# Inverse norms per sequence in ten GpSimd operations, and new instruction lists for a two-layer transformer kernel

## The reference

```
ada = silu(cond) @ Wada.T + bada          # gamma1, gamma2, scale1, scale2, shift1, shift2
qn = q / max(norm(q), 1e-12) * exp(min(scale_mul_log, log(100)))   # one factor per head
kn = k / max(norm(k), 1e-12)
o  = softmax(qn @ kn.T + attn_bias) @ v
x  = x + (o @ Wproj.T + bproj) * gamma1
x  = x + (gelu(ln(x)*(scale2+1)+shift2 @ Wfc1.T + bfc1) @ Wfc2.T + bfc2) * gamma2
```

## Time and profile before

| | before |
|---|---|
| median of 3 runs | 340.05 us |
| the 3 runs | 339.28, 340.05, 344.35 us |
| profiled execution, own time | 337.69 us |
| profiled execution, span from first to last instruction | 335.9 us |
| mean granted TensorE clock | 0.98 |
| busy PE, DVE, ACT, POOL | 301.0, 221.2, 207.0, 149.7 us |

### The profile page before, as it was taken

How to read it: one execution, slowest core, us unless ns; L and a number is a source line. 1 busy time by engine, 2 the same in 40 slices (tenths; PEclk the granted TensorE clock), 3 DMA queues, 4 the chain that set the end, 5 groups by cost and what they waited for, 6 DMA issues and landing times.

```text
span 335.9 us, 7317 instructions
## 1 busy us (share of the span) xinstructions
PE 301.0 (90%) x2516; PEld 251.2 (75%) x2516; DVE 221.2 (66%) x535; ACT 207.0 (62%) x698; POOL 149.7 (45%) x264
## 2 busy tenths in 40 slices
PE   7797766799987989986999999999979999999986
PEld 7396555576866866765797878889768898988985
DVE  3854788688777889858868688664453883543441
ACT  3454639989992899887699576836571433632110
POOL 3446959764475453688325138522214512202000
PEclk9599999999997999999999999999979999999999
DMA  6998223000000020000001000000000000000000
GB/s 200 283 338 283 83 92 126 1 2 3 1 2 2 0 65 0 3 1 3 0 2 64 0 2 2 2 0 18 8 12 0 2 0 18 17 2 19 16 0 33
DMA packets 14037, 14.30 MB, mean 43 GB/s; under 512 B 1569, under 2 KB 12961, under 8 KB 14001
## 3 DMA queue, kind: packets, MB, share of 16 engines
q1 hardware_dynamic: 14000, 13.83, 13.1%
HBM read 12.76 MB, written 1.06 MB: 41 GB/s over the span
## 4 chain that ended last, share of the span: by engine, by line
PE 54%; DVE 16%; POOL 9%; issue 8%; ACT 8%; DMA 3%; SPq 1%; DVEq 0%; POOLq 0%; ACTq 0%
PE ps_linear L1562 15%; PE ps_hidden L1366 6%; PE ps_hidden L1368 5%; PE ps_hidden L1367 5%; PE ps_linear L1532 3%; PE ps_probs L1497 3%; ACT z L980 3%; DMA stage<-in_Wqkv 3%; DVE z L1254 2%; PE ps_scores L1486 2%; PE ps_turn L1402 2%; DVE neg_max L1265 2%; PE ps_output L1513 2%; PE ps_turn L1396 1%; PE ps_scores L1481 1%
## 5 line engine op out<-in xcount | busy, mean ns | idle before, releaser
L980 ACT ACTIVATE z<-z,neg_max 128x128 f32<-128x128 f32 x128 | 49.6, 391 | 13.1 <-DVE neg_max L1265 12.9
L822 POOL TENSOR_TENSOR h_lo<-xn,h_hi 128x256 fp32r<-128x256 f32 x32 | 24.1, 756 | 40.9 <-ACT h_hi L944 40.8
L1000 ACT ACTIVATE probsT<-ps_probs 128x512 f32<-128x512 f32 x48 | 28.4, 591 | 11.3 <-PE ps_probs L1497 11.2
L1497 PE MATMUL ps_probs<-ident,z 128*128 128x128 f32 x192 | 29.9, 278 | 3.7 <-ACT probsT L1000 2.6
L1562 PE MATMUL ps_linear<-WdT,g_h 128*128 128x256 f32 x128 | 29.5, 383 | 1.4 <-DVE g_h L1337 1.3
L1036 ACT ACTIVATE g_a<-ps_hidden 128x256 f32<-128x256 f32 x32 | 12.4, 387 | 29.0 <-PE ps_hidden L1368 28.6
L874 POOL TENSOR_TENSOR z<-z,row_inv 128x512 f32<-128x512 f32 x16 | 17.0, 1062 | 28.1 <-DVE row_inv L1279 28.1
L1562 PE MATMUL ps_linear<-Wfc2T,g_h 128*128 128x256 f32 x128 | 29.4, 382 | 0.0
L1497 PEld LDWEIGHTS ps_probs<-ident,z 128*128 128x128 f32 x192 | 21.7, 141 | 7.7 <-ACT probsT L1000 3.7
L1562 PEld LDWEIGHTS ps_linear<-WdT,g_h 128*128 128x128 f32 x128 | 23.7, 190 | 5.0 <-issue 1.4
L984 ACT ACTIVATE z<-ps_scores,neg_max 128x128 f32<-128x128 f32 x64 | 22.6, 368 | 7.8 <-DVE neg_max L1271 7.8
(11 more groups left out here) (166 smaller groups left out, 897.5 us busy)
## 6 DMA issues: line engine op xcount, KB each, us to landing
gamma<-gamma_scratch SPq DMA_DIRECT2D x8, 256.0 KB, 3.8
stage<-in_Wada SPq DMA_DIRECT2D x6, 256.0 KB, 4.0
stage<-in_Wqkv SPq DMA_DIRECT2D x4, 256.0 KB, 4.9
X<-in_x SPq DMA_DIRECT2D x4, 256.0 KB, 5.3
stage<-in_Wfc SPq DMA_DIRECT2D x4, 256.0 KB, 5.8
Wfc2T<-in_Wfc SPq DMA_DIRECT2D x1, 1024.0 KB, 7.5
WdT<-in_Wd SPq DMA_DIRECT2D x1, 1024.0 KB, 8.5
stage<-in_Wg SPq DMA_DIRECT2D x4, 256.0 KB, 2.7
```

The source lines that it names most:

```text
L822: pool.tensor_tensor(h_lo[:, m, :, j * P:(j + 1) * P], h_full[:, m, j, :, :], h_hi[:, m, :, j * P:(j + 1) * P].bitcast(F32), ALU.subtract) ...
L980: ins = act.activation(z[:, d, u, :], z[:, d, u, :], ACT.Exp, bias=neg_max[:, d, u:u + 1], accum_out=head_sum[:, n % 2, t, u, b:b + 1])
L1000: act.activation(probsT[:, G % 2, :, :], bank_of(key)[:, :].rearrange("p (u q) -> p u q", u=4), ACT.Copy).then_inc(is_freed(key)[0], 1)
L1497: ins = pe.transpose(bank[:, u * P:(u + 1) * P], z[:, G % DEEP, u, :], ident[:, :])
```

## The change

First, `qk_root_` works on one sequence (32 columns) and takes ten operations: one of third order (six operations) and one Newton round (four). Second, the head scale moves into its input: `head_scale` now holds exp(-2 log scale) for q and 1 for k, and the floor operation on DVE multiplies by it, so that the inverse root comes out with the scale inside. The first `qk_sum` on DVE therefore waits for `head_exp` on ACT, which POOL waited for before. A sequence's inverse norms are no longer bound to those of its partner.

Third, the play's numbers change: a load 0.95 for 0.75, the DMA latency 3.0 for 2.2, other durations of a few steps, and all due times. Fourth, some steps are held back in the play until what reads them can follow: a QK product until its buffer is free, a V product until the last values that read its buffer, a transpose until the last scores of its kind, a projection until its gamma has come; and steps of one name keep their order.

```diff
+MIN_LOG_SCALE = -20.0
...
-NEWTON = 3
...
-GROUP_US = [-39.5, -38.5]
...
+GROUP_US = [-6.5, -554.0]
+ATT_BASE = [-3890.5, -875.0, -147.0, -2073.0, 1326.5, -859.0, 551.0, 1266.0]
+MLP_BASE = [374.5, 2507.0, -998.5, -79.5, -1090.5, -2655.5, 3581.0, -1914.5]
...
-LATENCY = 2.2
+LATENCY = 3.0
...
-    add(("sines",), "ACT", 4.0, [("angles", 2)], at=2)
-    add(("load_small",), "SP", 4.0, at=-3.3)
+        add(("angles", i), "DVE", (1.4, 1.25, 0.7)[i], [("cond_silu",)] + ([("angles", i - 1)] if i else []), at=2)
+    add(("sines",), "ACT", 2.0, [("angles", 2)], at=2)
+    add(("load_small",), "SP", 4.5, at=-3.3)
     add(("head_clip",), "DVE", 0.2, [("load_small",)], at=1)
-    add(("head_exp",), "ACT", 0.25, [("head_clip",), ("cond_tanh",)], at=1)
...
-        add(("load", c), "SP", 0.75, [user] if c >= STAGE else [], at=due)
+        add(("load", c), "SP", 0.95, [user] if c >= STAGE else [], at=due)
...
-                add(("qk_product", n), "PE", 1.55, [("norm_low", "a", n), w_ready], "linear", at=a)
+                add(("qk_product", n), "PE", 1.55, [("norm_low", "a", n), w_ready, last_j.get(("qk", j))], "linear", at=a)
...
-                add(("v_product", n), "PE", 0.8, [("norm_low", "a", n), ("qk_product", n), ("weight_low", LAST_CHUNK["Wqkv"])], "linear", at=a + 0.1)
+                add(("v_product", n), "PE", 0.8, [("norm_low", "a", n), ("qk_product", n), ("weight_low", LAST_CHUNK["Wqkv"]), last_values], "linear", at=a + 0.1)
...
-                add(("qk_sum", n), "DVE", 1.25, [("qk_square", n), last_j.get(("qk", j))], at=a)
+                add(("qk_sum", n), "DVE", 1.3, [("qk_square", n), ("head_exp",), last_j.get(("qk", j))], at=a)
+                add(("qk_root", n), "Pool", 3.5, [("qk_sum", n)], at=a)
+                add(("qk_scale", n), "DVE", 1.0, [("qk_root", n)], at=a)
...
-                    add(("qk_root", r), "Pool", 5.0, [("qk_sum", m) for m in ns] + [("head_exp",)], at=a)
...
-            add(("project", n), "PE", 0.95, [("attn_copy", n), ("load_whole", "Wproj" if layer == 0 else "Wo"), prev(("project",), n)], "linear", at=g)
+            add(("project", n), "PE", 0.95, [("attn_copy", n), ("load_whole", "Wproj" if layer == 0 else "Wo"), prev(("project",), n)]
+                + ([("gamma_load", pair)] if layer == 0 else []), "linear", at=g)
             add(("residual", "a", n), "DVE", 0.335, [("project", n), prev(("residual", "a"), n)]
...
+    last = {}
+    for key, step in steps.items():
+        name = key[:2] if len(key) > 2 and isinstance(key[1], str) else key[0]
+        if name not in ("load", "load_x", "load_whole", "gamma_load", "modulate", "modulated", "store"):
+            if name in last and last[name] not in step[2]:
+                step[2].append(last[name])
+            last[name] = key
...
+            pool.memset(head_scale[:, H0:2 * H0], 1.0)
...
-            def qk_root_(r):
-
-
-                o = ord0(2 * r) // 2
-                half, t, y = qk_half[:, :, :], qk_t[:, :, :], qk_r[:, :, :]
-                done = o * 4 * NEWTON
-                pool.wait_ge(qk_guess, 2 * o + 2)
-                pool.tensor_scalar(half, qk_fl[:, :, :], -0.5, None, ALU.mult)
-                for i in range(NEWTON):
-                    if i:
-                        pool.wait_ge(qk_root_step, done + 4 * i)
-                    pool.tensor_tensor(t, y, y, ALU.mult).then_inc(qk_root_step, 1)
-                    pool.wait_ge(qk_root_step, done + 4 * i + 1)
-                    pool.tensor_tensor(t, t, half, ALU.mult).then_inc(qk_root_step, 1)
-                    pool.wait_ge(qk_root_step, done + 4 * i + 2)
-                    pool.tensor_scalar(t, t, 1.5, None, ALU.add).then_inc(qk_root_step, 1)
-                    pool.wait_ge(qk_root_step, done + 4 * i + 3)
-                    pool.tensor_tensor(y, y, t, ALU.mult).then_inc(qk_root_step, 1)
-                pool.wait_ge(qk_root_step, done + 4 * NEWTON)
-                if o == 0:
-                    pool.wait_ge(scale_ready, 1)
-                pool.tensor_tensor(qk_r[:, :, 0:H0], qk_r[:, :, 0:H0],
-                                   head_scale[:, :].unsqueeze(1).to_broadcast([P, 2, H0]), ALU.mult).then_inc(qk_rnorm, 1)
+            def qk_root_(n):
+
+                o, j = ord0(n), n % 2
+                x, t, u, y = qk_fl[:, j, :], qk_t[:, j, :], qk_u[:, j, :], qk_r[:, j, :]
+                done = o * 9
+                pool.wait_ge(qk_guess, o + 1)
+                pool.tensor_tensor(t, y, y, ALU.mult).then_inc(qk_root_step, 1)
+                pool.wait_ge(qk_root_step, done + 1)
+                pool.tensor_tensor(t, t, x, ALU.mult).then_inc(qk_root_step, 1)
+                pool.wait_ge(qk_root_step, done + 2)
+                pool.tensor_scalar(u, t, 0.375, -1.25, ALU.mult, ALU.add).then_inc(qk_root_step, 1)
+                pool.wait_ge(qk_root_step, done + 3)
+                pool.tensor_tensor(t, t, u, ALU.mult).then_inc(qk_root_step, 1)
+                pool.wait_ge(qk_root_step, done + 4)
+                pool.tensor_scalar(t, t, 1.875, None, ALU.add).then_inc(qk_root_step, 1)
+                pool.wait_ge(qk_root_step, done + 5)
+                pool.tensor_tensor(y, y, t, ALU.mult).then_inc(qk_root_step, 1)
+                pool.wait_ge(qk_root_step, done + 6)
+                pool.tensor_tensor(t, y, y, ALU.mult).then_inc(qk_root_step, 1)
+                pool.wait_ge(qk_root_step, done + 7)
+                pool.tensor_tensor(t, t, x, ALU.mult).then_inc(qk_root_step, 1)
+                pool.wait_ge(qk_root_step, done + 8)
+                pool.tensor_scalar(t, t, -0.5, 1.5, ALU.mult, ALU.add).then_inc(qk_root_step, 1)
+                pool.wait_ge(qk_root_step, done + 9)
+                pool.tensor_tensor(y, y, t, ALU.mult).then_inc(qk_rnorm, 1)
 
...
-                act.activation(head_scale[:, :], head_log[:, :], ACT.Exp).then_inc(scale_ready, 1)
+                act.activation(head_scale[:, 0:H0], head_log[:, :], ACT.Exp, scale=-2.0).then_inc(scale_ready, 1)
...
-                dve.tensor_scalar(head_log[:, :], head_log[:, :], MAX_LOG_SCALE, None,
-                                  ALU.min).then_inc(scale_clipped, 1)
+                dve.tensor_scalar(head_log[:, :], head_log[:, :], MAX_LOG_SCALE, MIN_LOG_SCALE,
+                                  ALU.min, ALU.max).then_inc(scale_clipped, 1)
...
-                    dve.wait_ge(qk_rnorm, o // 2)
-                dve.tensor_scalar(qk_fl[:, j, :], qk_ss[:, j, :], NORM_FLOOR, None, ALU.max).then_inc(qk_floored, 1)
+                    dve.wait_ge(qk_rnorm, o - 1)
+                if o == 0:
+                    dve.wait_ge(scale_ready, 1)
+                    dve.wait_ge(consts_set, 2)
+                dve.scalar_tensor_tensor(out=qk_fl[:, j, :], in0=qk_ss[:, j, :], scalar=NORM_FLOOR,
+                                         in1=head_scale[:, :], op0=ALU.max, op1=ALU.mult).then_inc(qk_floored, 1)
 
                 dve.wait_ge(qk_floored, o + 1)
                 if o >= 2:
-                    dve.wait_ge(qk_normed, 2 * (o // 2))
+                    dve.wait_ge(qk_normed, o - 1)
...
-                dve.wait_ge(qk_rnorm, o // 2 + 1)
+                dve.wait_ge(qk_rnorm, o + 1)
...
```

More of the change, by code:

```diff
@@ L89 @@
-MLP_SPAN = [-295.5, 386.0]
+    'Wfc1': 3051.0, 'Wg': 4947.0, 'Wkv': -232.0, 'Wq': 8011.0, 'Wqkv': 3139.5, 'Wu': -4501.0, 'ada': 1911.5,
+    'tw1': -2373.0, 'tw2': -367.0}
+MLP_SPAN = [-1198.5, 1936.5]
 SHIFT = {
[L91 to L101, removed]
-    'row_inverse': 1112.5, 'row_max': -1805.5, 'scores': -397.0, 'sines': 391.5, 'store': 1349.0,
-    'sum_inverse': -962.0, 'tanh': -19.5, 'v_copy': -307.0, 'v_product': 1260.5, 'values': -69.5,
-    'weight_high': 592.0, 'weight_low': 626.0, ('norm_stats', 'a'): 285.5, ('norm_stats', 'm'): -665.0,
-    ('norm_root', 'a'): 136.0, ('norm_root', 'm'): -1064.0, ('norm_apply', 'a'): -644.5, ('norm_apply',
-    'm'): -450.5, ('norm_turn', 'a'): -712.5, ('norm_turn', 'm'): 265.5, ('norm_mod', 'a'): -873.0,
-    ('norm_mod', 'm'): 40.0, ('norm_high', 'a'): -363.0, ('norm_high', 'm'): -559.0, ('norm_low', 'a'):
-    -278.5, ('norm_low', 'm'): 436.5, ('residual', 'a'): -248.5, ('residual', 'm'): -49.0, ('residual_add',
-    'a'): 1035.0, ('residual_add', 'm'): 113.0}
@@ new lines @@
+    'warm': 900.0, 'angles': -2187.5, 'attn_copy': 408.5, 'cond_silu': 2646.0, 'cond_tanh': 268.5, 'down':
+    1119.0, 'exp': 3337.0, 'fc1': -2109.0, 'gamma_load': -3710.0, 'gamma_store': 470.5, 'gate': 868.5,
+    'gate_up': 2067.0, 'gelu': -2310.0, 'gelu_in': 1778.5, 'gelu_inner': 2225.5, 'head_clip': -1104.0,
+    'head_exp': 166.0, 'inv_copy': 1919.0, 'inv_spread': 370.0, 'inv_turn': -492.5, 'k_copy': 120.0,
+    'k_turn': 698.5, 'load': -1753.5, 'load_small': -943.0, 'load_whole': 1820.0, 'load_x': -2746.5,
@@ new lines @@
+    -5621.0, 'qk_sum': 3071.0, 'qkv1_copy': -2594.0, 'qkv1_product': 2597.5, 'residual': -1863.5,
+    'residual_add': 1116.5, 'rope': 946.5, 'row_inverse': 2355.0, 'row_max': -2133.0, 'scores': -2490.5,
```

(11 more changed lines are left out.)

40 lines of the change are left out of this document (16 added, 24 removed), and 3 rows, old and new, of the table SHIFT.

## The result

| | before | predicted | after |
|---|---|---|---|
| median of the runs beside each other | 341.21 (4 runs) | | 325.33 (4 runs, 324.39 to 326.22) |
| against before | | 0.962 | 0.953 [0.944, 0.961] |
| median | 340.05 | 327.0 | 325.33 |
| span of the profiled execution | 335.9 | 322.8 | 324.3 |
| its own time | 337.69 | 324.6 | 326.22 |

What follows compares the result with a forecast made beforehand. Bound by a latency chain up to 49.07, then ACT's exponentials to 89, then PE. Span 335.9 - 12.6 + 2.5 - 3 = 322.8; with 1.8 and 2.4 more, median 327.0; range 317 to 336.

Steps and rivals of the forecast that it cites:

- Start gained: From the start to the first exponential: it comes at 36.5 for 49.07, 12.6 sooner, bounds 33 and 42.
- the small loads hold the gain back: Between first product and roots: the last small load lands at 15, so the copy of product 0 runs at 15.2.
- X earlier is part of the gain: At the start: X of pair 0, third in SP's new list, is used at about 6.7 for 8.66, 2.0 sooner.
- The root: Root on POOL: ten operations at 32 columns take 3.6; `head_exp` and its table load cost nothing, with 0.8 of cover.
- 4.3 that the new order spends: POOL's list ahead of sequence 0's pack: a low half (0.75) and root 1 (3.6) stand before it, costing 4.3.
- The middle keeps its length, and the gain goes through: First exponential to first GELU input: ACT's stretch, 95% full, keeps its 41 and passes on the whole start gain.
- The rest, +2.5 - 3 = -0.5: Behind the first `fc1`: seven more fillers cost 2.5, lists holding products and transposes back are credited 3, between 0 and 6.
- Roots of later pairs at 0: Last three pairs of layer 0: first root ends 1.9 sooner, second 1.7 later, beside other rounds' exponentials, so 0.
- without that cover: Last three pairs of layer 0: if other rounds' exponentials did not lie beside the roots, 3 x 1.7 = 5.1 longer.
- Late small loads: Rival at the start: small loads land at 20, not 15, first exponential 41.5, median 335; chance 0.05.
- POOL as the gate: Rival in layer 0 pairs: first sequence's pack waits behind the second's root, 9.8 longer, start's gain lost, median 352.4; chance 0.05.
- DVE and POOL against each other: Rival at the start: DVE operations stretched beside POOL give half back, first exponential at 43, median 336.6; chance 0.16.

Runs made afterwards that it cites:

- the second profile: The changed kernel itself, nothing altered, profiled again in a second set of runs: 0.956 [0.952, 0.961] against the kernel before, span 323.1.
- the sixteen copies: Changed kernel with sixteen unread copies added on ACT, two ahead of each of the first eight groups of exponentials: 329.77, 0.970 against the kernel before.
- the kernel with thirteen operations: Changed kernel with its lists, but each sequence's inverse root in 13 operations for ten: 332.05, 0.976 against the kernel before.
- the four fillers ahead of each modulation product: Changed kernel with 12 more fillers, four ahead of each of modulation products 7, 8, 9, and product 10 behind QK product 2: 325.82, 0.958 against the kernel before.

## Why the prediction held, step by step

- **Start gained: right in kind, too large by 3.5,** or by 2.1 in the second profile: 9.0 and 10.5 for 12.6. 2.9 of the 3.5, and 1.5 of the 2.1, are there when the first root starts. Not counted were two queues on DVE (the norm ahead of copy 0, copy 1 ahead of the sum), which both profiles have, and the first product at half clock, which only the first has. The step "the small loads hold the gain back" was wrong: the copy ran at 17.21 and 16.18 behind other work.
- **X earlier is part of the gain: wrong.** With the old load order the kernel is as fast.
- **The root: right.** 3.26 for 3.6, and `head_exp` cost nothing, though its cover was 0.1 and not 0.8. A drain behind the table load did not show in either load.
- **"4.3 that the new order spends": wrong.** To take it back cost 5.
- **The middle keeps its length, and the gain goes through: right here,** 40.55 and 39.10 for 40.81, and the sixteen copies show ACT as the bound. But it is not so for every set of lists and roots: with the old roots in the new lists the stretch took 47.3, with the first pack moved ahead 43.5.
- **The rest, +2.5 - 3 = -0.5:** counted from the first `fc1` it was -1.0 and +0.8, counted from the GELU input -2.3 and -0.6, so the total is not shown to be off. Its terms were: the fillers cost 0.6, and PE's idle time did not fall. There is a gain ahead of the first `down`, from the GELU input to there: 18.7 before, 14.4 and 14.5 now. Of this 1.9 and 3.6 are lost again further on, in the second profile 1.7 of them in that `down` itself.
- **Roots of later pairs at 0: the step that failed most.** I allowed 5.1 "without that cover", and found the first root 1.9 sooner against the second 1.7 later to be even. Three more operations per root cost 6.7, and sharing the root again cost 14.9. The root of a sequence on its own is what lets the pack of the third pair's first sequence be done early.
- **The rivals.** Late small loads: excluded by the start. POOL as the gate: its place was right and its sign was wrong. POOL does gate the third pair, and the pair is faster, because the first root is no longer part of that queue. DVE and POOL against each other: single rows are stretched (an operation of 0.18 took 1.18 at 76.62, beside a weight half of POOL at 76.46 to 77.75). Here the Trainium skill (SBUF — State Buffer, "SBUF: two separate sides"), by which one holds the shared port for a whole instruction, agrees with the row: DVE's operation ended when POOL's had. How much of the 3.5 it is was not taken apart. That rival's median, 336.6, lay outside the range up to 336 that was to take in most of it.

What was off, the start by 3.5 and 2.1 too much and all behind the first exponential by some 2 too little (2.6 and 2.3 gained for 0.5), partly cancelled. That the forecast was closer than its steps is luck.

Open stays what the holds, the due times and the other changed numbers of the play are worth alone, and which of the queues would have to move to make the changed kernel faster. Of the moves tried, none beats it by more than the intervals.

## What to carry to other kernels

In statically ordered lists an engine's idle time is a property of the lists, not of the work: when the lists change, ask anew which engine is full ahead of each milestone. A shorter operation and a new order can each be worth nothing and together 4.7%, so measure both alone before crediting one. Take two profiles of the same kernel before reading a difference of 1 or 2 between milestones: here they differed by up to 2.9. Where a walk through the start ends sooner than everything else, add the instruction ahead in each engine's queue before naming a transfer as the limit.

## What was not expected of the hardware

The first `down`, 16 matmuls, took 3.67 to 3.69 in nine of the fourteen profiles, the change's first among them, and 5.38 in the other five, the change's second among them. Busy time and clock of PE, just ahead of the first `down` of the kernel with thirteen operations, and during it:

```profile
96.00:99.00 3.00, 1.33 (x14) 1.00 0.02 5
99.00:104.50 5.50, 5.40 (x20) 0.69 0.00 0
```

PE had been 44% busy, and the granted clock was 0.69 in the stretch that followed, part of it at 1.2 GHz. In the change's first profile PE was as idle ahead of its first `down` and kept its clock, so the rows don't tell when it falls. It takes 1.7 and so can take back what an earlier start brings.

Another fall came while PE was busy. PE's timeline of the change at 24.71, 24 modulation matmuls whose moving operand has 8 columns, without a gap, and the same 24 in its second profile:

```profile
24.71 3.85 PE L1396 MATMUL ps_hidden<-cols,stage 128*128 128x8 f32 x24
23.33 2.96 PE L1396 MATMUL ps_hidden<-cols,stage 128*128 128x8 f32 x24
```

PE in stretches there (length, busy time and instructions, clock, DMA), the first two rows of the first profile and the third of the second:

```profile
24.00:26.00 2.00, 2.00 (x20) 1.00 0.60 170
26.00:28.00 2.00, 2.00 (x13) 0.53 0.95 277
26.00:28.00 2.00, 2.00 (x13) 1.00 0.91 287
```

PE is busy throughout in all three rows. The same matmuls in the same list ran into the lower clock in one execution and kept the full one in the other. So the four fillers ahead of each modulation product, with which the clock was 1.00 there too, are not shown to be what kept it. A stretch that reads as full can be at the lower clock, so both columns are to be read. Behind 26 it cost nothing, as the time from the first root to the first exponential shows; between 10 and 18 two profiles with such a fall took 0.7 and 1.6 longer up to the first root than the change's second profile.
